# Causal mask of the maximum on the vector engine, 65 columns a tile in one output bank, three work banks

## The reference

```python
q = (rms_norm(x @ w_qa) @ w_qb)          # 16 heads, 128 plain and 64 rotary features
c_kv, k_rope = split(x @ w_kva)          # one latent of 64 and one rotary key of 64 for all heads
scores = einsum('bhsd,bhtd->bhst', q_full, k_full) / sqrt(192)
scores = where(tril, scores, finfo.min)
attn = softmax(scores)
out = einsum('bhst,bhtd->bhsd', attn, v) ; out = out.reshape(b, seq, H * 128) @ w_o
```

## Time and profile before

| | us |
|---|---|
| median of 3 runs (lowest to highest) | 1313.97 (1307.87 to 1314.54) |
| the profiled execution, its own time | 1310.41 |
| its span, first to last instruction | 1308.6 |
| PE busy | 1182.8 |
| PE weight loads busy | 948.0 |
| DVE busy | 880.5 |
| ACT busy | 789.5 |
| POOL busy | 692.6 |

### The profile page before, as it was taken

The page is one execution under the profiler, slowest core; times in us unless marked ns, Lnnn a source line. Parts: engine busy times, 40 slices in busy tenths (PEclk is TensorE's granted clock), DMA queues, the critical chain, the costliest instruction groups (busy, mean ns, idle before and its releaser), DMA issues. The chain is left out here.

```text
span 1308.6 us, 23936 instructions
## 1 busy us (share of the span) xinstructions
PE 1182.8 (90%) x9452; PEld 948.0 (72%) x9452; DVE 880.5 (67%) x1836; ACT 789.5 (60%) x1166; POOL 692.6 (53%) x569
## 2 busy tenths in 40 slices
PE   2856899999999999999999999999999867989897
PEld 2644577777777777777767777777878766878786
DVE  2533776677686777767677776767766567677776
ACT  1163467777777777777777777777787733222232
POOL 0121366767767666776766777666676742111100
PEclk9875699999999999999999999999999987999999
DMA  9202010000100200010020010002000050000000
GB/s 275 81 1 57 17 42 12 7 17 18 42 17 2 58 2 17 27 32 17 2 58 1 17 38 22 18 1 58 2 17 2 1 161 1 1 17 1 17 17 17
DMA packets 57679, 39.65 MB, mean 30 GB/s; under 512 B 7744, under 2 KB 57152, under 8 KB 57408
## 3 DMA queue, kind: packets, MB, share of 16 engines
q1 hardware_dynamic: 51216, 33.94, 8.8%
q10 hardware_dynamic: 6352, 4.19, 1.4%
HBM read 33.66 MB, written 4.46 MB: 29 GB/s over the span
## 5 line engine op out<-in xcount | busy, mean ns | idle before, releaser
L793 DVE TENSOR_REDUCE gates<-bank 128x1 f32<-128x512 f32 (+3 forms) x640 | 380.5, 608 | 210.4 <-PE bank L866 135.4
L685 POOL TENSOR_TENSOR pt_lo<-pt 128x1024 f16<-128x1024 f32 x192 | 375.2, 1964 | 213.4 <-ACT pt L742 213.3
L742 ACT ACTIVATE pt<-pair 128x1024 f32<-128x1024 f32 x192 | 196.2, 1022 | 131.0 <-PE pair L895 130.6
L733 ACT ACTIVATE pair<-shift 128x1024 f32<-128x1024 f32 x256 | 263.7, 1030 | 12.2 <-ACT pt L746 0.4
L909 PE MATMUL bank<-values,pt_lo 128*128 128x65 f16 x2176 | 225.4, 193 | 8.2 <-DVE rowsum L825 7.4
L911 PE MATMUL bank<-values,pt 128*128 128x129 f16 x2176 | 232.2, 220 | 0.0
L909 PEld LDWEIGHTS bank<-values,pt_lo 128*128 128x128 f16 x2176 | 185.4, 98 | 48.9 <-issue 27.9
L691 POOL TENSOR_TENSOR pt_lo<-pt 128x512 f16<-128x512 f32 (+3 forms) x256 | 179.1, 722 | 64.9 <-ACT pt L746 63.7
L911 PEld LDWEIGHTS bank<-values,pt 128*128 128x128 bf16 x2176 | 193.3, 98 | 0.0
L746 ACT ACTIVATE pt<-pair 128x512 f32<-128x512 f32 (+3 forms) x256 | 110.6, 436 | 63.8 <-PE pair L895 52.8
L895 PE MATMUL pair<-q_hi,kt_a_hi 128*128 128x512 f32 (+1 forms) x320 | 135.4, 423 | 0.0
(11 more groups left out here) (217 smaller groups left out, 2306.0 us busy)
## 6 DMA issues: line engine op xcount, KB each, us to landing
turn_by<-rope_cos_by_feature SPq DMA_DIRECT2D x64, 128.0 KB, 3.0
turn_by<-rope_sin_by_feature SPq DMA_DIRECT2D x64, 128.0 KB, 3.0
xs<-in_L_attn_x ACTq DMA_DIRECT2D x1, 2048.0 KB, 25.4
lat<-in_L_attn_w_o SPq DMA_DIRECT2D x1, 2048.0 KB, 26.6
xs_again<-in_L_attn_x SPq DMA_DIRECT2D x1, 2048.0 KB, 8.1
out<-xs_again SPq DMA_DIRECT2D x4, 512.0 KB, 2.8
lat<-in_L_wmod SPq DMA_DIRECT2D x1, 1536.0 KB, 15.9
lat<-in_L_attn_w_qb SPq DMA_DIRECT2D x1, 1152.0 KB, 8.1
```

Source lines behind the costliest of these rows:

```text
L685: pool.tensor_tensor(out=pt_lo[:, at].rearrange("p a n -> p (a n)"), in0=full, in1=cut(full), op=ALU.subtract).then_inc(low_ok, 1)
L733: act.activation(s_pair[u % 2][:, :, :], shift[:, item % SHIFTS:item % SHIFTS + 1, :].to_broadcast([P, 2, BW]), ACT.Copy).then_inc(seeded[ ...
L742: act.activation(pt[:, at], s_pair[u % 2][:, :, :], ACT.Exp).then_inc(exp_done, 1)
L793: dve.tensor_reduce(out=mx[:, item % MAXIMA, t, part:part + 1], in_=work_of(w)[:, 0:n * P], axis=AXX, op=ALU.max).then_inc(work_seen["v"], 1)
```

## The change

The mask of the maximum is no longer a matmul. For chunks on the diagonal DVE takes, in place of the reduction, `tensor_tensor_reduce`: it adds a row of the mask to the scores in the bank, writes the sum back to the bank and gives the maximum of it. `mask16` grows to 512 columns, zero but for the last 128, and a chunk of n tiles uses the last n x 128 of it. The order of the chunks is the plain one again.

The values product is three matmuls for each tile pair, of 65, 64 and 65 columns: high part by high values and ones, high part by low values, low part by high values and ones. All add to the same 65 columns, four tiles of 65 in one bank. So `evacuate` is one copy for each item, after its last unit, and `lat` has 65 columns for each head: `rowsum` is gone, and `experts` reads both out of `lat`. The freed bank makes `work_bank` three banks: PE waits for use n - 3.

```diff
-for _k in range(NI):
-    _at = range(FIRST_CHUNK[_k], FIRST_CHUNK[_k + 1])
-    _rest = [CHUNKS[c] for c in _at if CHUNKS[c][2] != ITEMS[_k][1]]
-    _diagonal = [CHUNKS[c] for c in _at if CHUNKS[c][2] == ITEMS[_k][1]]
-    _places = sorted(_at, key=lambda c: not before_values(c))[:BT]
-    for _c in _at:
-        CHUNKS[_c] = (_diagonal if _c in _places else _rest).pop(0)
...
-        lat = sb(stack, "lat", [P, NT, H * KVL])
+        lat = sb(stack, "lat", [P, NT, H * (KVL + 1)])
-        mask16 = sb(attn, "mask16", [P, P], BF16)
+        mask16 = sb(attn, "mask16", [P, BW], BF16)
-    o_bank, work_bank = bank[4:6], bank[6:8]
+    o_bank, work_bank = bank[4], bank[5:8]
...
-            return work_bank[n % 2]
+            return work_bank[n % 3]
...
-                    dve.tensor_reduce(out=mx[:, item % MAXIMA, t, part:part + 1], in_=work_of(w)[:, 0:n * P], axis=AXX,
-                                      op=ALU.max).then_inc(work_seen["v"], 1)
+                    of, to = work_of(w)[:, 0:n * P], mx[:, item % MAXIMA, t, part:part + 1]
+                    if part == ITEMS[item][1]:
+                        dve.tensor_tensor_reduce(out=of, in0=of, in1=mask16[:, BW - n * P:], scale=1.0, scalar=LOWEST, op0=ALU.add,
+                                                 op1=ALU.max, accum_out=to).then_inc(work_seen["v"], 1)
+                    else:
+                        dve.tensor_reduce(out=to, in_=of, axis=AXX, op=ALU.max).then_inc(work_seen["v"], 1)
...
-                    dve.tensor_reduce(out=lat[:, tiles, head * KVL:head * KVL + KVL],
-                                      in_=of[:, :, 0:2 * KVL].rearrange("p t (a n) -> p t n a", a=2), axis=AXX,
-                                      op=ALU.add).then_inc(o_seen, 1)
-                    dve.tensor_copy(rowsum[:, tiles, head:head + 1], of[:, :, 2 * KVL:2 * KVL + 1]).then_inc(o_seen, 1)
+                    dve.tensor_copy(lat[:, BT * g:BT * g + BT, head * (KVL + 1):head * (KVL + 1) + KVL + 1],
+                                    o_bank[:, 0:BT * (KVL + 1)].rearrange("p (t n) -> p t n", t=BT)).then_inc(o_seen, 1)
...
-                    if r >= 2 and UNITS[r - 2][2] is not None:
+                    if r >= 2 and UNITS[r - 2][2] == 2:
                         evacuate(r - 2)
...
-                    wait_seen(pe, w - 2)
+                    wait_seen(pe, w - 3)
-                    last = pe.matmul(to[:, 0:cols], q, kt_hi[h][:, part * BW:part * BW + cols], start=True, stop=not diagonal)
-                    if diagonal:
-                        last = pe.matmul(to[:, (n - 1) * P:n * P], ident16[:, :], mask16[:, :], start=False, stop=True)
-                    last.then_inc(work_done, 1)
+                    pe.matmul(work_of(w)[:, 0:cols], q, kt_hi[h][:, part * BW:part * BW + cols], start=True,
+                              stop=True).then_inc(work_done, 1)
...
-                        pe.wait_ge(o_seen, 4 * item)
+                        pe.wait_ge(o_seen, item)
...
-                            pe.matmul(to[:, col + KVL:col + 2 * KVL + 1], pt_lo[:, at, half, mine], values[:, j + half, KVL:2 * KVL + 1],
-                                      start=(u == FIRST_UNIT[item] and half == 0 and t % 2 == 0), stop=False, skip_group_check=True)
-                            last = pe.matmul(to[:, col:col + 2 * KVL + 1], cut(pt[:, at, half, mine]),
-                                             values[:, j + half, 0:2 * KVL + 1], start=False, stop=end, skip_group_check=True)
+                            low_values, with_one = values[:, j + half, 0:KVL], values[:, j + half, KVL:2 * KVL + 1]
+                            pe.matmul(to, cut(pt[:, at, half, mine]), with_one, start=(u == FIRST_UNIT[item] and half == 0 and t == 0),
+                                      stop=False, skip_group_check=True)
+                            pe.matmul(to[:, 0:KVL], cut(pt[:, at, half, mine]), low_values, start=False, stop=False,
+                                      skip_group_check=True)
+                            last = pe.matmul(to, pt_lo[:, at, half, mine], with_one, start=False, stop=end, skip_group_check=True)
...
-                    pool.tensor_tensor(out=lat_n[:, t % 2], in0=lat[:, tile, :].rearrange("p a (h n) -> p (a h) n", h=H),
+                    pool.tensor_tensor(out=lat_n[:, t % 2], in0=lat[:, tile, :].rearrange("p a (h n) -> p (a h) n", h=H)[:, :, 0:KVL],
```

More of the change, by code:

```diff
@@ L42 @@
 BW = BT * P
+MASK_AT = BW - P
 SCALE = 1.0 / math.sqrt(DN + DR)
@@ L45 @@
 MASKED = -1.0e30
+LOWEST = -3.0e38
 P_SCALE = 1024.0
@@ L93 @@
 assert len(SHIFT_AT) == len(ITEM_MAX_AT) == NI and len(PREP_AT) == 4 * len(PAIRS)
-def before_values(c):
-    r = CHUNK_ROUND[c]
-    return c == CHUNKS_AT[r][-1] and len(CHUNKS_AT[r]) > 1 and r not in SHIFT_AT and PREP_AT.get(r, (0, 3))[1] == 3
-for _k in range(NI):
-    _at = range(FIRST_CHUNK[_k], FIRST_CHUNK[_k + 1])
-    _rest = [CHUNKS[c] for c in _at if CHUNKS[c][2] != ITEMS[_k][1]]
-    _diagonal = [CHUNKS[c] for c in _at if CHUNKS[c][2] == ITEMS[_k][1]]
-    _places = sorted(_at, key=lambda c: not before_values(c))[:BT]
-    for _c in _at:
-        CHUNKS[_c] = (_diagonal if _c in _places else _rest).pop(0)
 WORK_ORDER = []
@@ L141 @@
 SEEDS = {e: [0, *itertools.accumulate(seed_on_vector(u) == (e == "v") for u in range(NU))] for e in "av"}
-ENDS = [0, *itertools.accumulate(d is not None for _, _, d in UNITS)]
 def adaln_block_kernel(nc, x, w_qa, q_norm, w_qb, w_kva, kv_norm, w_kvb, w_o, w_gate, wi_0, wi_1, wo, c, wmod,
@@ L315, in _ @@
                                        pattern=[[-1, P]], channel_multiplier=1).then_inc(consts, 1)
-                pool.affine_select(out=mask16[:, :], in_=mask16[:, :], compare_op=ALU.is_ge, fill=MASKED, base=0,
+                pool.affine_select(out=mask16[:, MASK_AT:], in_=mask16[:, MASK_AT:], compare_op=ALU.is_ge, fill=MASKED, base=0,
                                    pattern=[[-1, P]], channel_multiplier=1).then_inc(consts, 1)
@@ L592, in attend @@
 def attend(nc, sb, sem, k):
-    bank, lat, rowsum, ident, wq_dram, values = k["bank"], k["lat"], k["rowsum"], k["ident"], k["wq_dram"], k["values"]
+    bank, lat, ident, wq_dram, values = k["bank"], k["lat"], k["ident"], k["wq_dram"], k["values"]
     ident16, mask16 = k["ident16"], k["mask16"]
@@ L847, in query_products @@
                         pe.wait_ge(wq_in, 32 * loads)
-                    if n >= 2:
-                        wait_seen(pe, n - 2)
+                    if n >= 3:
+                        wait_seen(pe, n - 3)
                     w = [wq[a][:, part * P:part * P + P] for a in range(2)]
@@ L863, in maximum @@
                     cols = max(n * P, 2 * P)
-                    to, diagonal = work_of(w), part == g
                     q = q_hi[:, item // 2 % Q_SLOTS, h, t * P:t * P + P]
-                    last = pe.matmul(to[:, 0:cols], q, kt_hi[h][:, part * BW:part * BW + cols], start=True, stop=not diagonal)
-                    if diagonal:
-                        last = pe.matmul(to[:, (n - 1) * P:n * P], ident16[:, :], mask16[:, :], start=False, stop=True)
-                    last.then_inc(work_done, 1)
+                    pe.matmul(work_of(w)[:, 0:cols], q, kt_hi[h][:, part * BW:part * BW + cols], start=True,
+                              stop=True).then_inc(work_done, 1)
                 def shift_rows(item):
                     n = WORK[("shift", item)]
-                    wait_seen(pe, n - 2)
+                    wait_seen(pe, n - 3)
                     pe.wait_ge(spread_ok, item + 1)
@@ L885, in scores @@
                             on = (d + n) * P
-                            pe.matmul(s_pair[u % 2][:, n, on:on + P], mask16[:, :], ident16[:, :], start=False, stop=False,
+                            pe.matmul(s_pair[u % 2][:, n, on:on + P], mask16[:, MASK_AT:], ident16[:, :], start=False, stop=False,
                                       skip_group_check=True)
@@ L905, in weigh @@
                         for t in range(0 if d is None else d + half, BT):
[L906 removed]
+                            to = o_bank[:, t * (KVL + 1):t * (KVL + 1) + KVL + 1]
                             mine = slice(t * P, t * P + P)
                             end = d is not None and t == d + half
[L909 to L912 removed]
+                            low_values, with_one = values[:, j + half, 0:KVL], values[:, j + half, KVL:2 * KVL + 1]
[4 more added lines that the diff above has]
+                            last = pe.matmul(to, pt_lo[:, at, half, mine], with_one, start=False, stop=end, skip_group_check=True)
                     last.then_inc(pv_done, 1)
@@ L940, in experts @@
 def experts(nc, sb, sem, k):
-    bank, lat, rowsum, ident, gates = k["bank"], k["lat"], k["rowsum"], k["ident"], k["gates"]
+    bank, lat, ident, gates = k["bank"], k["lat"], k["ident"], k["gates"]
     modc, neg_half, turnstile = k["modc"], k["neg_half"], k["turnstile"]
@@ L1272, in _ @@
                 for tiles in (slice(0, BT), slice(BT, NT)):
```

(2 more changed lines are left out.)

4 lines of the change are left out of this document (removed).

## The result

The changed kernel takes 1255.35 us (median of 4 runs, 1254.86 to 1255.61), against 1313.1 us (4 runs) for the kernel before on the same chip: 0.9569 of it, 95% interval 0.9547 to 0.9591. Forecast were 1267 us, 1248 to 1300. The profiled execution took 1254.86 us. Its span fell by 55.5 us, where the sum had -47.

What follows compares the result with a forecast made beforehand. The attention stage was taken as bound by TensorE's columns, small fixed costs and waits. Terms of -53 us, 6 given back, made -47 from the profiled 1310.4: 1263, then 1267 because the median runs 0.3% higher; range 1248 to 1300.

Steps and rivals of the forecast that it cites:

- third values matmul: Values product: 2176 pairs become triples of the same 194 columns, +2.5 ns each, +5 us.
- one output bank, one evacuation: Evacuation: one 260-column copy per item replaces two reductions and two copies; first values matmuls wait less, -5 us.
- third bank, in the units: Attention units: one more bank use ahead covers the late maxima, removing TensorE's waits for work banks, -30 us.
- third bank, ahead of them: Before the units: the first two query groups wait less for VectorE, 1 to 1.5 us each, -3 us.
- mask: 256 mask matmuls leave TensorE: 143 ahead of values matmuls save 7 us, 113 between fp32 matmuls 13, together -20 us.
- plain order: Chunks return to natural order, which mattered only to the masks' place: 0 us.
- given back to waits on ScalarE and POOL: Attention stage: ScalarE and POOL keep their work as it shortens, so waits on them now show, +6 us.
- What bounds the kernel: Attention stage: TensorE bound by columns plus small fixed costs, plus waits; afterwards over 97% busy, stage 48 to 50 us shorter.
- Rival 2: Values product: third matmul doesn't fit, loads or issue have a floor; 1357 us (chance 0.09) or 1295 to 1308 (0.08).
- DVE's load: VectorE in the stage: evacuation saves 45 us, masked maxima add 41, ending at 628 us and hidden as before.
- Rival 3: VectorE becomes the bound: add with maximum takes two passes, 81% busy, the bank gain of 30 goes; 1297 us, chance 0.08.
- Rival 4: TensorE's waits only change name, to ScalarE's seeds and exponentials; only matmul work counts, -15, 1299 us, chance 0.05.

Runs made afterwards that it cites:

- c1: Kernel before with only the values product changed, to three matmuls (65, 64, 65 columns); mask on TensorE and two work banks kept: 1322.86 us.
- c2: c1 plus one output bank with one evacuation copy per item; still two work banks and the mask on TensorE: 1315.82 us.
- c3: c2 plus the freed bank as third work bank, waits for use n - 3; mask still on TensorE: 1267.4 us.
- a3: Changed kernel with the chunk order of the kernel before put back (diagonal chunks last in a round where possible): 1249.12 us.
- a2: Changed kernel with two work banks again in place of three, waits for use n - 2; all else as changed: 1314.09 us.
- a5: Changed kernel with item_shift moved behind the evacuation in VectorE's rounds: 1247.3 us.
- n2: Changed kernel with a plain reduction for every chunk and no mask in the maximum on either engine: 1247.95 us.
- c4: Kernel before with its two values matmuls in swapped order, 129 columns first and 65 last; nothing else: 1317.21 us.

## Why the prediction was right

The direction, the bound and the chief term were right. The sum was less good than it looks: the third bank alone brought 20 us more than forecast, everything else together took 12 of them back, and the span fell by 8.5 us more than the -47. That errors of both signs met is luck. The median beat the forecast by 11.7; the other 3 us are those that I had added between profiled execution and median, which in the kernel after lie 0.5 us apart. The terms of the sum, and what the stage of the nearest pair of profiles says:

| term | forecast | measured |
|---|---|---|
| third values matmul | +5 | +11.4 (c1) |
| one output bank, one evacuation | -5 | -3.5 (c2 to c1) |
| third bank, in the units | -30 | -45.5 (c3 to c2) |
| third bank, ahead of them | -3 | -8.0 (c3 to c2), some 4 of it with the clock |
| mask | -20 | -17.0 (a3 to c3) |
| plain order | 0 | +1.4 (after to a3) |
| given back to waits on ScalarE and POOL | +6 | not separated |
| sum | -47 | -61.2 |

The span shows -55.5: ahead of the units 2.2 us came back with the mask on DVE (34.1 us in a3 against 31.9 in c3, but with 29.8 us at 1.2 GHz against 22.9, so it need not be the mask), the untouched rest added 4.7 and `prepare` took 1.4 less. The terms depend on the order in which they are taken: the third bank is worth 45.5 us in the stage with the mask on TensorE (c2, c3) and 57.1 with it on DVE (a2, after).

- **What bounds the kernel.** Right: c2 to c3 changes waits alone and brings the greatest part. TensorE is busy for 99% of the stage; the forecast "over 97%" was a weak sign, since it was 97.4% before.
- **The third bank** was the mis-sized term, -33 for -53.5. The step that failed is the count of distances "over 150 ns too long, 41 us together": it left out what comes behind a late start, in the query products and in front of the values, and all small excesses. Of the 45.5 us, 31.8 were in distances over 150 ns too long (36.7 us in c2, 4.9 in c3), and 5.4 of these stood in front of values matmuls, where the wait is for the evacuation; the other 13.6 were in shorter ones. That one use ahead covers the late reader was right; no wait of L837 or L856 for L782 is over 0.3 us in after. Ahead of the units the stretch is 8 us shorter in place of 3, but less the clock's estimated 4 the ring's share is close to the forecast; which of its uses there gained, I did not separate.
- **The third matmul** was mis-sized the other way. The triple is 0.093 us on average in c1 where 0.088 to 0.090 was said, and 4 ns a pair instead of 2.5 makes 8.6 instead of 5 us. The step that failed is to multiply a median by the count: the mean, 3.8 ns, stood in the trace of before and gives 8.3. The other 5 us were not in the sum: I had costed a matmul by its successor of its own kind, and not the last one of a product, ahead of an fp32 load. Rival 2 (24 ns a triple turn the sign) is out by far.
- **The mask** was right in size, within 3 us, but only in the company of the third bank: with two banks it is worth 4.0 us. Where TensorE waits for DVE anyway, work taken off TensorE lengthens the wait, and the masked maximum lies ahead of that wait: from c2 to a2 the distances over 150 ns too long grew from 36.7 to 47.9 us and the wait for the evacuation from 9.6 to 14.6. Terms that I had added were not independent.
- **The evacuation.** -5 was near in size (-3.5) and wrong in its reason. PE's wait for it is 10.5 us in the earlier trace rows, 10.2 in c1, 9.6 in c2, 4.2 in c3, 8.3 in a3 and 9.9 in after. So the shorter evacuation left the wait nearly as it was, and what c2 gained lies before `shift_rows`. The third bank halved the wait, and the masked maxima, put in DVE's program ahead of the evacuation, took that back. a5 shows that it was the place in the round that mattered. "Hides as it did" held for DVE's sum, and not for this one deadline (n2: 5.6 us).
- **DVE's load.** Forecast 628 us, measured 597. The masked maxima were right one by one (0.70 and 0.14 us), but the small instruction starts 0.61 us after the first, before its end, so durations must not be added. They add 11 us of busy time (581.0 in c3, 591.7 in a3) and not 41. The evacuation's saving is 30 us (c1 to c2) and not 45, for the same reason: its durations fell by 45 us, but they had overlapped each other and their neighbours. The rest is mostly the multiply L804 (L792 after), 61 of them: 1056 ns in c2, 780 in c3 and 881 in after.
- **The accumulator.** The Trainium skill ("VectorE: DVE Perf Modes", Two Vector instructions with no wait between them) has an operation that writes its accumulator as two instructions; the trace agrees, with 239 reads of 139 ns in the groups above.
- **Rival 3.** Out: an add with maximum takes 0.70 us at 512 columns, as its nearest row did, and not over 1.2, and DVE ends at 71% of the stage.
- **Rival 4.** Out: the bank waits went and nothing of their size came. Waits for the low parts (L669, L675) are 16.1 us in the list now and 8.4 in c3, in weight loads that lie partly behind a running matmul. No run takes them away, so what the 6 us given back came to stays open.

What made the evacuation late, the traces show. L804's multiply, which has both operands in SBUF, takes 0.69 us at least, and in before 16 of the 61 took over 0.8 us, up to 2.41. Each of these 16 began while a GpSimd instruction ran and ended 0.55 us after that one's end, and so did each of the 13 over 0.8 us in after. The one of the earlier trace rows ends at 569.86; GpSimd had on record, until 569.31:

```profile
566.78 2.53 POOL L677 TENSOR_TENSOR q_lo<-qf,q_hi 128x512 fp32r<-128x512 f32 x2 [0.21 <-ACT q_hi L715]
```

So it waits for GpSimd, and how often differs from kernel to kernel: 16 of these in c2, 10 in c3, 20 in a2. Another 20 multiplies of before began beside a GpSimd instruction and were not held, and no run changes this alone; what decides it stays open. The 4 ns a pair are measured, their cause is not.

## What to carry to other kernels

Before taking work off the bounding engine, see whether it waits in turn: here the same edit was worth 4 us with a ring of two banks and 17 with three, and the third bank alone 45.5 in the stage. The sum of waits over a threshold was a lower bound for what the deeper ring brought, because a late start also left the next load open. Price many small distances by their mean, not their median. And when work is moved to an engine with room on average, look for the one instruction behind it that has a deadline, and put that first.

## What the runs showed of the hardware

- Loads and matmuls of 64 and 65 columns run at three pairs in 0.093 (c1) to 0.094 us (after) on average, with no floor seen at 30 ns.
- An fp32 matmul of 512 columns behind a values matmul sets in equally late whether that has 65 or 129 columns: 0.35 and 0.34 us from its start to the second score matmul. Putting the short one last costs 4.4 us in the stage by itself (c4).
- An untouched stretch of 258 us became 263 when 49 us of it in place of 31 were at 1.2 GHz, and edits that don't touch it moved it by as much (c2 to c3 +6.2 us, after to a3 -4.3 us). The kernel before shows it too: of its 19 runs beside c1, four took 1307.6 to 1309.1 us at a mean clock of 0.959 to 0.960, the others 1311.3 to 1314.7 us at 0.954 to 0.958. Of the ten runs of c2 three took 1320.6 to 1322.3 us at 0.954, the others 1314.6 to 1317.3 at 0.962 to 0.966. Differences of under 5 us between kernels say little without that window.
- A DVE multiply of two SBUF operands, 0.69 us by itself, took up to 2.41 us where it began during a GpSimd instruction; every one over 0.8 us ended 0.55 us after that instruction's end (16 in before, 13 in after).
- A DVE instruction that writes its accumulator is followed by a 0.14 us read that starts before the first ends: 242 of them in the stage of a3 added 11 us of busy time to c3's, where the durations sum to 36.
